# First-layer attention with keys on partitions: scores in column tiles, row sums by a matmul, reciprocals through DRAM

## Chip, cores and metric

One core of a Trainium2 chip runs the whole program. The metric is the device time of one execution in microseconds (us).

## The reference

Two transformer layers over x (16 batches x 64 tokens x 512). Only the first layer's cross-attention is touched:

```
q = rope(layernorm(x) @ Wq)          32 heads x 128
k = rope(ctx @ Wk), v = ctx @ Wv      8 key heads x 128, four query heads share one
logits = 30 * tanh((q . k) * 0.0884 / 30)          per batch 64 x 64
weights = softmax(where(mask, logits, -1e30))       the mask is the same for all rows and batches
x = x + (weights @ v) @ Wo
x = x + lora_experts(layernorm(x))                  first layer's FFN
x = x + attention2(layernorm(x), ctx)               16 heads x 96
x = x + dense(layernorm(x))
```

The given mask is true where a key is padding, and the reference keeps the logits where it is true. A row with no true entry gets equal weights.

## The kernel before

`plan()` writes one list of steps; each engine's program (`sync_program`, `gpsimd_program`, `scalar_program`, `vector_program`, `tensor_program`) walks the list in that order and does its own part of every step, so a wait on an engine holds everything that stands behind it in the list. A semaphore per PSUM bank says full and another free. Banks 0, 1, 6, 7 are a ring in the loop; bank 2 (PS) holds scores, bank 3 (PT) transposes, banks 4 and 5 (PA) the product with V.

Projections are done to nearly fp32 accuracy with three fp32r matmuls per product (`thrice`, lines 976 to 978): weights and activations are split in a high and a low part. A `split` step loads 256 KB of weights through one of four stage buffers (SP, line 519), writes the high part on ScalarE (line 603) and the low part on GpSimd (line 569). fp32 matmuls (scores, P·V) leave two records each in the trace.

The first layer's attention loop has NS = 32 steps s, each for two query heads (unit u = s // 2) and one half of the batch (s % 2, 8 batches). Per step:

- q0, 2 tiles of 12 matmuls with 512 columns (line 976 ff.); rope in three VectorE multiplications (lines 827, 828, 830) and a GpSimd addition (578) into `qb`;
- b0, scores: per batch a matmul of 64 columns, queries of two heads on the partitions (line 1031); tanh on ScalarE (645), mask on VectorE (847), exp on ScalarE (647), row sum, reciprocal and normalization on VectorE (852, 854, 856), all in `Eb`;
- c0: four 128x128 transposes (983) to PT and a ScalarE copy to `pTb`;
- d0, P·V: 8 matmuls with 64 rows in two row tiles (1050), 128 columns each, into the two PA banks; high part on ScalarE (603), low part on VectorE (865);
- e0: 4 tiles of 6 matmuls with Wo (976 ff.), each added to `xs` on VectorE (760).

The loop runs them in a software pipeline: iteration it issues b0(it-1), q0(it), d0(it-2), e0(it-3), c0(it-1), with splits, keys k0 and values v0 strewn in. Before the loop the first half of x and ctx (LO) is normalized, transposed and projected, then the second (HI). There the list reads: stats and rstd of HI (VectorE lines 778 to 800), q0(0), mask_bias (834 to 840), k0(0,1), transposes and values of HI.

```
for it in range(NS + 2):
    if 0 <= it - 1 < NS: stage("b0", it - 1, bank=2)
...
    if 0 < it < NS: q0(it)
...
    if 0 <= it - 2 < NS: d0(it - 2)
...
    if 0 <= it - 3 < NS: e0(it - 3)
...
    if 0 <= it - 1 < NS: stage("c0", it - 1, bank=3)
```

Of the kernel before, what the change touches and what calls it, by code (L numbers as in the profile page):

```python
# [7 lines left out]
NS = 32  # L8
# [54 lines left out]
def plan():  # L63
# [3 lines left out]
    def split(*name):  # L67
        step("split", *name)
# [28 lines left out]
    def q0(s):  # L97
        for n in range(2):
            stage("q0", s, n)

    def d0(s):
        for w in range(2):
            tile("d0", s, w, bank=4 + w)
        step("d0", s)

    def e0(s):
        for c in range(4):
            stage("e0", s, c)
# [12 lines left out]
    split("wq0", 0)  # L121
    split("wq0", 1)
# [18 lines left out]
    for it in range(NS + 2):  # L141
        if 0 <= it - 1 < NS:
            stage("b0", it - 1, bank=2)
        if it % 4 == 0 and it // 4 + 1 < 8:
            split("wk0", it // 4 + 1)
        if it % 8 == 1 and it // 8 + 1 < 4:
            for c in range(2):
                split("wv0", it // 8 + 1, c)
        if it % 2 == 0 and it // 2 + 1 < 16:
            split("wq0", it + 2)  # L150
        if it % 2 == 1 and it < NS:
            split("wo0", it - 1)
        if 0 < it < NS:
            q0(it)
        if it == NS + 1:
            k1(0, 0, 0)
        if 0 <= it - 2 < NS:
            d0(it - 2)
        if it % 2 == 1 and it + 2 < 32:
            split("wq0", it + 2)  # L160
        if 0 <= it - 3 < NS:
            e0(it - 3)
        if it % 2 == 0 and 2 <= it <= NS:
            split("wo0", it - 1)
        if it % 4 in (1, 2) and it // 4 + 1 < 8:
            stage("k0", it // 4 + 1, it % 4 - 1)
        if 3 <= it % 8 <= 6 and it // 8 + 1 < 4:
            for i in range(2):
                v0(it // 8 + 1, 2 * (it % 8 - 3) + i)
        if 0 <= it - 1 < NS:  # L170
            stage("c0", it - 1, bank=3)
        if it == NS - 2:
            split("wk1", 0, 0)
        if it == NS - 1:
            split("wv1", 0)
            split("wv1", 1)
        if it == NS:
            split("wq1", 0, 0)
            split("wq1", 0, 1)
        if it == NS + 1:  # L180
            split("wv1", 2)
            split("wq1", 0, 2)
            step("ffn_load")
# [33 lines left out]
    e0(NS - 1)  # L217
# [100 lines left out]
def program(nc, a, out):  # L318
# [18 lines left out]
    with ExitStack() as ctx:  # L337
# [9 lines left out]
        arena = sb("arena", [128, 10240])  # L347
# [3 lines left out]
        rtmp = [arena[:, 6144 + s * 512:6144 + (s + 1) * 512] for s in range(2)]  # L351
        K1 = [arena[0:96, j * 2048:(j + 1) * 2048] for j in range(4)]
        w1T = arena[:, 8192:10240].rearrange("p (k n) -> p k n", k=4)
# [7 lines left out]
        Ol = sb("Ol", [128, 2, 2, 512], f32r)  # L361
        Ohp, Olp = (O[:, :, :, :].rearrange("p s n t -> p s (n t)") for O in (Oh, Ol))
# [13 lines left out]
        mbias = sb("mbias", [128, 64])  # L376
        many = sb("many", [128, 1])
# [14 lines left out]
        with nc.sbuf_tensor("cTh", [128, 4, 1024], f32r) as cTh, nc.sbuf_tensor("cTl", [128, 4, 1024], f32r) as cTl:  # L392
# [5 lines left out]
        mids = [bank[:, 0:272].rearrange("p (i n) -> p i n", i=4) for bank in (PS, PT)]  # L398
        wk_home = [(WKh[:, :], WKl[:, :]), (WOh[:, 1, :], WOl[:, 1, :])]
        wk1_at = {(0, 0): 0, (1, 0): 1, (2, 0): 0, (0, 1): 0, (1, 1): 0, (2, 1): 0}  # L400
        wv1_home = [(WVh[:, 0:384], WVl[:, 0:384]), (WVh[:, 512:896], WVl[:, 512:896]),
                    (WOh[:, 2, 0:384], WOl[:, 2, 0:384]), (WOh[:, 0, 0:384], WOl[:, 0, 0:384])]
# [19 lines left out]
        s_msk, s_exp, s_sum, s_rec, s_nrm = (sem(n) for n in ("masked", "exp", "rowsum", "rowrec", "probs"))  # L422
        s_ohi, s_ohi1 = sem("o_hi"), sem("o_hi1")
        s_mb = sem("mask_bias")
# [836 lines left out]
```

## Time and profile before

| | |
|---|---|
| median of 3 runs | 926.53 us (925.81 to 926.71) |
| profiled execution | 922.79 us, span 921.0 us, granted TensorE clock 0.994 |
| TensorE matmul busy | 890.2 us, 97% |
| TensorE weight load busy | 757.1 us, 82% |
| VectorE, ScalarE, GpSimd busy | 583.4, 375.2, 270.5 us |
| HBM | 38.7 MB by SP's DMA queue |

Matmul records are pipelined: one of 512 columns lasts 0.39 us and the next starts 0.23 after it. The first layer's attention loop runs from about 43 to 579 us, its FFN to about 620, the second layer to the end. A granted clock of 1.00 is 2.4 GHz on TensorE.

### The profile page before, as it was taken

What the parts mean: (1) busy time and instruction counts of PE and PEld (TensorE: products, weight loads), DVE (VectorE), ACT (ScalarE), POOL (GpSimd) and SP (SyncE); (2) the same over time, 40 slices, a digit from 0 to 9 for tenths busy, and PEclk for the clock granted to TensorE, in tenths of its full rate; (3) what the DMA queues carried; (4) which work ended last, traced back from release to release, by engine and by line L of the source; (5) the groups of instructions that cost most, each with busy time, mean ns of one, the idle gap of its engine ahead of it and who ended that gap; (6) DMA issues with size and microseconds to landing.
All of it is one profiled execution on the core that took longest, in us unless ns stands there. A gap on an engine that the chain in (4) does not pass through costs nothing.

```text
span 921.0 us, 13308 instructions
## 1 busy us (share of the span) xinstructions
PE 890.2 (97%) x5144; PEld 757.1 (82%) x5144; DVE 583.4 (63%) x1035; ACT 375.2 (41%) x875; POOL 270.5 (29%) x212
## 2 busy tenths in 40 slices
PE   5889999999999999999999999799999999999998
PEld 5778888888888888888888888669987888888776
DVE  6886765876765876765877776753134454555684
ACT  4533222313222323222322223446576767766642
POOL 3263323533323533323433333100021211102132
PEclk9999999999999999999999999899999999999999
DMA  8021101211101211101111112100010110210002
GB/s 291 1 81 36 46 24 35 69 29 29 46 23 35 69 27 32 47 23 35 46 28 43 32 32 87 35 3 10 12 46 24 35 47 24 94 45 1 1 1 92
DMA packets 21888, 39.56 MB, mean 43 GB/s; under 512 B 2944, under 2 KB 3840, under 8 KB 21696
## 3 DMA queue, kind: packets, MB, share of 16 engines
q1 hardware_dynamic: 21824, 38.70, 13.9%
q8 instruction: 41, 0.67, 0.3%
q14 instruction: 23, 0.19, 0.1%
HBM read 36.60 MB, written 2.10 MB: 42 GB/s over the span
## 4 chain that ended last, share of the span: by engine, by line
PE 81%; DVE 7%; ACT 7%; issue 2%; POOL 1%; DMA 1%; SPq 0%; DVEq 0%; POOLq 0%
PE PB L976 20%; PE PB L978 19%; PE PB L977 19%; PE PB L1031 6%; PE PB L1122 5%; PE PB L1050 4%; PE PB L983 3%; ACT Eb L728 2%; PE PB L1137 2%; PE PB L1154 2%; DVE Ol L947 1%; ACT Oh L603 1%; DVE st L778 1%; DVE sm L929 1%; ACT qb L718 1%
## 5 line engine op out<-in xcount | busy, mean ns | idle before, releaser
L760 DVE TENSOR_TENSOR xs<-xs,PB 128x512 f32<-128x512 f32 x176 | 114.8, 682 | 35.6 <-PE PB L978 32.0
L976 PE MATMUL PB<-WOh,Oh 128*128 128x512 f32 x320 | 128.0, 400 | 0.0
L978 PE MATMUL PB<-WOh,Ol 128*128 128x512 f32 x320 | 125.0, 391 | 0.0
L977 PE MATMUL PB<-WOl,Oh 128*128 128x512 f32 x320 | 124.8, 390 | 0.0
L603 ACT ACTIVATE Oh<-PB 128x512 fp32r<-128x512 f32 (+2 forms) x160 | 71.0, 465 | 131.3 <-PE PB L1050 113.2
L578 POOL TENSOR_TENSOR qb<-qb,arena 128x512 f32<-128x512 f32 x64 | 82.9, 1295 | 108.2 <-DVE arena L830 108.2
L976 PE MATMUL PB<-xTh,WQh 128*128 128x512 f32 x256 | 102.8, 402 | 2.0 <-DVE xTl L807 2.0
L978 PE MATMUL PB<-xTh,WQl 128*128 128x512 f32 x256 | 100.0, 391 | 0.0
L977 PE MATMUL PB<-xTl,WQh 128*128 128x512 f32 x256 | 99.8, 390 | 0.0
L569 POOL TENSOR_TENSOR WOl<-stage,WOh 128x512 fp32r<-128x512 f32 (+1 forms) x43 | 54.8, 1276 | 144.4 <-ACT WOh L603 140.5
L569 POOL TENSOR_TENSOR WQl<-stage,WQh 128x512 fp32r<-128x512 f32 x44 | 59.9, 1364 | 98.6 <-ACT WQh L603 72.0
L847 DVE SCALAR_TENSOR_TENSOR Eb<-Eb,many,mbias 128x512 f32<-128x512 f32 x32 | 29.2, 913 | 81.2 <-ACT Eb L645 81.2
L976 PEld LDWEIGHTS PB<-WOh,Oh 128*128 128x128 f32 x320 | 60.0, 188 | 15.4
L603 ACT ACTIVATE pTb<-PB 128x512 f32<-128x512 f32 (+1 forms) x74 | 43.8, 592 | 65.7 <-PE PB L983 64.7
L978 PEld LDWEIGHTS PB<-WOh,Ol 128*128 128x128 f32 x320 | 60.1, 188 | 12.7
L977 PEld LDWEIGHTS PB<-WOl,Oh 128*128 128x128 f32 x320 | 60.1, 188 | 11.7
L983 PE MATMUL PB<-ident_sb,Eb 128*128 128x128 f32 x384 | 57.8, 275 | 11.1 <-DVE Eb L934 5.6
L947 DVE TENSOR_TENSOR Ol<-PB,Oh 96x256 fp32r<-96x256 f32 (+1 forms) x96 | 40.4, 421 | 41.8 <-ACT Oh L603 40.7
L1031 PE MATMUL PB<-arena,qb 128*128 128x64 f32 x512 | 60.8, 272 | 2.5 <-POOL qb L578 2.5
L728 ACT ACTIVATE Eb<-PB,sm 128x128 f32<-128x128 f32 x128 | 45.3, 366 | 43.5 <-DVE sm L929 43.5
L1031 PEld LDWEIGHTS PB<-arena,qb 128*128 128x128 f32 x512 | 59.7, 192 | 2.9 <-issue 2.9
L983 PEld LDWEIGHTS PB<-ident_sb,Eb 128*128 128x128 f32 x384 | 45.5, 141 | 19.0 <-DVE Eb L934 6.9
(152 smaller groups left out, 1892.0 us busy)
## 6 DMA issues: line engine op xcount, KB each, us to landing
stage<-in_wq SPq DMA_DIRECT2D x44, 256.0 KB, 2.6
stage<-in_wo SPq DMA_DIRECT2D x44, 256.0 KB, 2.6
stage<-in_wk SPq DMA_DIRECT2D x14, 256.0 KB, 2.6
arena<-in_ctxT SPq DMA_DIRECT2D x8, 256.0 KB, 5.7
xs<-in_x SPq DMA_DIRECT2D x8, 256.0 KB, 6.5
stage<-in_wv SPq DMA_DIRECT2D x8, 256.0 KB, 3.7
out<-xs SPq DMA_DIRECT2D x8, 256.0 KB, 2.0
arena<-in_w SPq DMA_DIRECT2D x1, 1024.0 KB, 5.2
```

The source lines that it names most:

```text
L569: e.tensor_tensor(lo, staged[:, n % 4, 0:cols], hi.bitcast(f32), ALU.subtract).then_inc(s_wlo)
L578: e.tensor_tensor(dst, dst, tmp, ALU.add).then_inc(s_radd)
L603: return e.activation(dst, src, ACT.Copy)
L728: last = e.activation(Eb[:, e2, cols], PS[:, cols], ACT.Exp, bias=mx[:, bb:bb + 1], accum_out=rs[:, bb:bb + 1])
L760: e.tensor_tensor(xs[:, i, :], xs[:, i, :], PB[b][:, :], ALU.add).then_inc(free[b])
L947: last = e.tensor_tensor(dl, src, dh.bitcast(f32), ALU.subtract)
L976: e.matmul(dst, Ah, Bh, start=(k == 0), stop=False)
L977: e.matmul(dst, Ah, Bl, start=False, stop=False)
L978: return e.matmul(dst, Al, Bh, start=False, stop=(k == n - 1))
L983: last = e.transpose(dst[:, c * 128:(c + 1) * 128], src[:, c * 128:(c + 1) * 128], ident[:, :])
L1031: last = e.matmul(PS[:, c * 64:(c + 1) * 64], qb[:, s % 2, c * 128:(c + 1) * 128], kT[j % 2][:, 512 * hf + 64 * c:512 * hf + 64 * c + 64], ...
L1122: last = e.matmul(PB[b][:, :], W[:, m, r], H[:, c, cols], start=(n % 12 == 0), stop=(n % 12 == 11))
```

## The change

A step is now a unit of four query heads, all that share one key head, and one half of the batch: NU = 16. Each unit has two halves h of four batches.

- b0: the key block is the stationary operand, the queries of four heads (256 columns) move. The result has 64 key rows; two batches fill the two column tiles of 64, four matmuls a half. Softmax's numerator then lies with keys on partitions, as P·V wants it, so c0 is gone.
- The mask is folded in two tables on the host-transposed mask: `ropeq` (rope times 1 or 0, so that logits become 0 if no key is kept) and `keep` (1 or 0 per key and query), which GpSimd multiplies after exp. Their making (`mask_tables`) uses a matmul with ones into bank 3, ahead of q0(0).
- sum0: four matmuls a half with a stationary `ones` of 32 columns and 128 moving columns, each in its own column tile of 32, into PT; VectorE takes the reciprocal of 128 x 128; SP writes the four useful rows for each of two batch parities to DRAM (`recs`), waits, and reads them back spread over 64 partitions (`rsum`); VectorE multiplies (norm0).
- d0: per half 4 matmuls of 256 columns. e0: one tile per 128 tokens sums four heads: 48 matmuls a unit as before in two steps, with 4 additions to xs instead of 8.
- Four weight slots instead of three for Wq and Wo; `w1T` gets room of its own. Four wq0 splits stand ahead of the first k0 (before two), and wk0(1), wv0(1), wo0(0..3) ahead of the loop.

```diff
@@ plan()
-    split("wq0", 0)
-    split("wq0", 1)
+    for n in range(4):
+        split("wq0", n)
     stage("k0", 0, 0)
...
     step("rstd", 0, 4)
-    q0(0)
-    step("mask_bias")
+    tile("many", bank=3)
+    step("mask_tables")
+    for n in range(4):
+        q0(0, n)
     stage("k0", 0, 1)
+    split("wk0", 1)
     normed(0, HI, [lambda i=i: v0(0, i) for i in range(5, 8)], [lambda: v0(0, 4)])
...
+    for c in range(2):
+        split("wv0", 1, c)
+    for n in range(4):
+        split("wo0", n)
+    for u in range(NU):
+        def queries(n):
+            if u + 1 < NU:
+                q0(u + 1, n)
+                if u % 2 == 0 and u + 2 < NU:
+                    split("wq0", 2 * u + 4 + n)
+        def outputs(c):
+            if u:
+                e0(u - 1, c)
+        b0(u, 0)
+        queries(0)
+        if u == NU - 1:
+            k1(0, 0, 0)
+        b0(u, 1)
+        queries(1)
+        sum0(u, 0)
+        outputs(0)
+        sum0(u, 1)
+        outputs(1)
+        norm0(u, 0)
+        queries(2)
+        norm0(u, 1)
+        queries(3)
+        d0(u, 0)
+        outputs(2)
+        outputs(3)
+        if u and u % 2 == 0:
+            for n in range(4):
+                split("wo0", 2 * u + n)
+        d0(u, 1)
+        j, hf = u // 2 + 1, u % 2
+        if j < 8:
+            stage("k0", j, hf)
...
     ring[0:0] = [4, 5]
-    e0(NS - 1)
+    for c in range(4):
+        e0(NU - 1, c)
@@ sync_program
+                elif kind == "sum0":
+                    u, h = k
+                    n, s = 2 * u + h, h
+                    sp.wait_ge(*read("sum0", u, h))
+                    if u:
+                        sp.wait_ge(s_in_rec[s], 32 * u)
+                    for bb in range(2):
+                        e.dma_start(recs[s, bb], rec[16 * bb:128:32, s, :]).then_inc(s_out_rec[s], 16)
+                    sp.wait_ge(s_out_rec[s], 32 * (u + 1))
+                    if u:
+                        sp.wait_ge(s_nrm, n - 1)
+                    for bb in range(2):
+                        e.dma_start(rsum[s][64 * bb:64 * bb + 64, :].rearrange("p (g x) -> p g x", g=4),
+                                    recs[s, bb].unsqueeze(0).broadcast_to([64, 4, 128])).then_inc(s_in_rec[s], 16)
@@ gpsimd_program
+                elif kind == "b0":
+                    u, h = k
+                    n = 2 * u + h
+                    E3 = E0[n % 4].rearrange("p (c t) -> p c t", c=8)
+                    pool.wait_ge(s_mb, 4)
+                    pool.wait_ge(s_exp, n + 1)
+                    e.tensor_tensor(E3, E3, keep[:, :].unsqueeze(1).broadcast_to([128, 8, 64]), ALU.mult).then_inc(s_msk)
@@ vector_program
+                elif kind == "mask_tables":
+                    dve.wait_ge(s_mask, 16)
+                    dve.wait_ge(s_rope, 16)
+                    e.tensor_copy(keep[:, :], mask8).then_inc(s_mb)
+                    dve.wait_ge(*done("many"))
+                    e.tensor_scalar(many[:, :], PT[:, 0:64], 1.0, None, ALU.min).then_inc(free[3])
...
+                elif kind == "sum0":
+                    u, h = k
+                    dve.wait_ge(*done("sum0", u, h))
+                    if u:
+                        dve.wait_ge(s_out_rec[h], 32 * u)
+                    e.reciprocal(rec[:, h, :], PT[:, 0:128]).then_inc(free[3])
+                elif kind == "norm0":
+                    u, h = k
+                    E = E0[(2 * u + h) % 4]
+                    dve.wait_ge(s_in_rec[h], 32 * (u + 1))
+                    e.tensor_tensor(E, E, rsum[h], ALU.mult).then_inc(s_nrm)
@@ tensor_program
+                elif kind == "mask_tables":
+                    pe.wait_ge(s_one, 1)
+                    pe.wait_ge(s_mb, 1)
+                    e.matmul(PT[:, 0:64], pTb[:, 0, 0:128], keep[:, :], start=True, stop=True).then_inc(full[3])
                 elif kind == "b0":
-                    for c in range(8):
-                        last = e.matmul(PS[:, c * 64:(c + 1) * 64], qb[:, s % 2, c * 128:(c + 1) * 128],
-                                        kT[j % 2][:, 512 * hf + 64 * c:512 * hf + 64 * c + 64], start=True, stop=True)
+                    for c in range(2):
+                        for r in range(2):
+                            b8 = 4 * h + 2 * c + r
+                            last = e.matmul(PS[64 * r:64 * r + 64, 256 * c:256 * c + 256],
+                                            kT[j % 2][:, 512 * hf + 64 * b8:512 * hf + 64 * b8 + 64],
+                                            qb[:, u % 2, 256 * b8:256 * b8 + 256], start=True, stop=True)
-                elif kind == "c0":
-                    s, = k
-                    pe.wait_ge(s_nrm, s + 1)
-                    turn(PT, Eb[:, s % 2, :], 4).then_inc(full[b])
+                elif kind == "sum0":
+                    for c in range(4):
+                        last = e.matmul(PT[32 * c:32 * c + 32, 0:128], ones[:, :],
+                                        E0[n % 4][:, 128 * c:128 * c + 128], start=True, stop=True)
                 elif kind == "d0":
+                    for c in range(2):
...
+                        for r in range(2):
...
+                            last = e.matmul(PA[r][:, 256 * c:256 * c + 256], V[rows, i, c0:c0 + 128],
+                                            E0[n % 4][rows, 256 * c:256 * c + 256], start=True, stop=True)
                 elif kind == "e0":
+                    for n in range(4):
+                        last = thrice(PB[b][:, :], n, 4, O4h[:, n, rows], O4l[:, n, rows], *wo_home[n])
```

## Rows read from the trace of the kernel before

**Rows 1.** The windows of the trace: stretch, its us, busy us of each engine (instructions), granted clock, DMA
```profile
160.00:240.00 80.00, 80.00 (x465) 67.32 (x464) 59.84 (x86) 22.23 (x41) 34.48 (x26) 1.00 0.15 43
...
580.00:600.00 20.00, 14.54 (x86) 12.50 (x85) 12.51 (x42) 11.79 (x20) 3.48 (x3) 0.83 0.14 40
```

**Rows 2.** Timeline of one step of the loop, TensorE: start us, us, instruction
```profile
302.79 0.39 PE L978 MATMUL PB<-xTh,WQl 128*128 128x512 f32 x1
...
303.11 1.16 PE L1050 MATMUL PB<-pTb,arena 64*128 64x128 f32 x16
...
304.20 0.50 PE L976 MATMUL PB<-WOh,Oh 128*128 128x512 f32 x1
...
304.54 0.39 PE L977 MATMUL PB<-WOl,Oh 128*128 128x512 f32 x1
...
309.55 0.39 PE L978 MATMUL PB<-WOh,Ol 128*128 128x512 f32 x1
...
309.78 0.60 PE L983 MATMUL PB<-ident_sb,Eb 128*128 128x128 f32 x4
...
310.22 1.90 PE L1031 MATMUL PB<-arena,qb 128*128 128x64 f32 x16
...
311.92 0.48 PE L976 MATMUL PB<-xTh,WQh 128*128 128x512 f32 x1
```

**Rows 3.** Timeline, second layer's scores, 96 rows, 128 columns
```profile
701.07 1.06 PE L1137 MATMUL PB<-arena,qb 96*128 96x128 f32 x8
701.88 0.48 PE L1122 MATMUL PB<-xTh,WQh 128*128 128x512 f32 x1
```

**Rows 4.** Chain that ended last, eight records of 512 columns
```profile
607.27 3.63 PE PB L1087 x8
```

**Rows 5.** Groups by line, busy us, mean ns: softmax instructions
```profile
L856 DVE TENSOR_TENSOR Eb<-Eb,sm 128x512 f32<-128x512 f32 x32 | 45.6, 1426 | 1.1
...
L854 DVE RECIPROCAL sm<-sm 128x8 f32<-128x8 f32 x32 | 6.5, 203 | 1.1
...
L932 DVE RECIPROCAL sm<-sm 128x4 f32<-128x4 f32 x32 | 5.7, 178 | 50.8 <-ACT Eb L728 50.8
```

**Rows 6.** The page's part 6, DMA issues: KB each, us to landing
```profile
stage<-in_wq SPq DMA_DIRECT2D x44, 256.0 KB, 2.6
...
arena<-in_ctxT SPq DMA_DIRECT2D x8, 256.0 KB, 5.7
...
out<-xs SPq DMA_DIRECT2D x8, 256.0 KB, 2.0
```

**Rows 7.** Timeline, TensorE's waits at the start
```profile
25.74 0.47 PE L976 MATMUL PB<-xTh,WQh 128*128 128x512 f32 x1 [1.78 <-DVE xTl L807]
...
42.34 0.66 PE L983 MATMUL PB<-ident_sb,Eb 128*128 128x128 f32 x4 [1.11 <-DVE arena L830]
...
56.15 1.97 PE L1031 MATMUL PB<-arena,qb 128*128 128x64 f32 x16 [2.31 <-POOL qb L578]
```

**Rows 8.** Timeline, VectorE at the start
```profile
15.98 1.20 DVE L796 TENSOR_TENSOR lnb<-lnb 128x4 f32<-128x4 f32 x1
...
34.28 0.16 DVE L800 SCALAR_TENSOR_TENSOR lnb<-mv,lnb 128x4 f32<-128x4 f32 x1
...
38.60 0.20 DVE L834 CAST mbias<-mask 128x64 f32<-128x64 uint8 x1
```

**Rows 9.** Timeline, GpSimd at the start
```profile
14.64 2.52 POOL L569 TENSOR_TENSOR WQl<-stage,WQh 128x512 fp32r<-128x512 f32 x2
```

**Rows 10.** Timeline, TensorE: first matmul after the last e0, and the FFN's wait
```profile
578.94 0.39 PE L976 MATMUL PB<-cTh,WKh 128*128 128x512 f32 x1
...
593.05 1.09 PE L983 MATMUL PB<-ident_sb,Eb 128*128 128x128 f32 x4 [4.27 <-ACT Eb L624]
```

**Rows 11.** Timeline, VectorE, additions after the last e0
```profile
579.95 2.47 DVE L760 TENSOR_TENSOR xs<-xs,PB 128x512 f32<-128x512 f32 x4
```

More of the change, by code:

```diff
@@ L95, in v1, with q0, b0, sum0 @@
         stage("v1", w, i)
[L97 to L101, printed above, removed]
-        for w in range(2):
[L103 to L108, printed above, removed]
+    def q0(u, n):
+        stage("q0", u, n)
+    def b0(u, h):
+        stage("b0", u, h, bank=2)
+    def sum0(u, h):
+        stage("sum0", u, h, bank=3)
+    def norm0(u, h):
+        step("norm0", u, h)
+    def d0(u, h):
+        for w in range(2):
+            tile("d0", u, h, w, bank=4 + w)
+        step("d0", u, h)
+    def e0(u, c):
+        stage("e0", u, c)
     split("wk0", 0)
@@ L346, in program @@
         xTl = sb("xTl", [128, 4, 1024], f32r)
-        arena = sb("arena", [128, 10240])
+        arena = sb("arena", [128, 8192])
+        with nc.sbuf_tensor("W3", [128, 4, 512], f32r) as W3:
+            more = [W3[:, n, :] for n in range(4)]
+        w1T = sb("w1T", [128, 4, 512])
         kT = [arena[:, s * 1024:(s + 1) * 1024] for s in range(2)]
@@ L636, in scalar_program @@
                     else:
[L637 removed]
+                        act.wait_ge(*done("d0", 4 * (pr - 2) + 3, 1, 1))
                     b = bank_of("v0", pr, i)
@@ L1047, in tensor_program @@
+                    for c in range(2):
+                        i = 4 * hf + 2 * h + c
+                        pe.wait_ge(*read("v0", j // 2, i))
                         for r in range(2):
-                            pe.wait_ge(*opened("d0", s, r))
+                            pe.wait_ge(*opened("d0", u, h, r))
                             rows = slice(64 * r, 64 * r + 64)
-                            last = e.matmul(PA[r][:, c * 128:c * 128 + 128], V[rows, 4 * hf + c, c0:c0 + 128],
-                                            pTb[rows, e2, c * 128:(c + 1) * 128], start=True, stop=True)
@@ L1059, in tensor_program @@
-                    pe.wait_ge(*read("d0", s, 1))
-                    pe.wait_ge(*lo_ready("wo0", 2 * u + 1))
-                    for n in range(2):
-                        slot = (2 * u + n) % 3
-                        last = thrice(PB[b][:, :], n, 2, Oh[:, e2, n, rows], Ol[:, e2, n, rows], WOh[:, slot, :], WOl[:, slot, :])
+                    pe.wait_ge(*read("d0", u, c // 2, 0))
+                    pe.wait_ge(*read("d0", u, c // 2, 1))
+                    pe.wait_ge(*lo_ready("wo0", 4 * (u // 2) + 3))
```

241 lines of the change are left out of this document (109 added, 132 removed).

## The prediction, made before the result was known

> **What bounds the kernel.** I read the windows first. In the first layer's attention loop TensorE is busy 80.00 of 80.00 us at granted clock 1.00, VectorE 59.84, GpSimd 34.48, ScalarE 22.23 [rows 1]. Matmuls are pipelined, so a busy row proves no peak, but there is no gap: every start follows the one before. The loop is priced by start-to-start times on TensorE, and time taken from another engine brings nothing there. So I read one step of the timeline [rows 2]. From 304.54 to 309.55 lie 22 starts of 512-column fp32r matmuls, 0.228 each. The step's fp32 stages are: P·V (L1050) 303.11 to 304.20, 1.09 us for 16 records; four transposes (L983) 309.78 to 310.22, 0.44; scores (L1031) 310.22 to 311.92, 1.70 for 16 records. Each fp32 matmul leaves two records, so half a matmul is a record below. Entering P·V costs 0.32 - 0.23 = 0.09 (302.79 to 303.11), leaving it 0.34 - 0.23 = 0.11 (304.20 to 304.54).
>
> **The loop, part by part.** A unit (4 heads, one half of the batch) replaces two steps; there are 16. The projections, 48 q0 and 48 e0 matmuls a unit, stay, and so do keys and values. Removed from TensorE per unit: scores 3.40, transposes 0.88, P·V 2.18, entries and exits 2 x (0.09 + 0.11) = 0.40, and leaving the scores about 0.09 each, which I take as 0.18 like the entry: together 7.04 us.
>
> Added: scores are 8 matmuls, 16 records, of 256 columns and 64 outputs, pairs of which sit in different column halves of the array. No row of before shows a column tile. Prices of 256 full-array columns: 128 columns took (701.88 - 701.07)/8 = 0.101 a record [rows 3], 512 took 3.63/8 = 0.454 [rows 4], so 256 stand near 0.227, or 0.213 counted from two passes at 2.4 GHz. If the two tiles of a pair run one after another, 16 records are 3.63. If they run together as the row tiles of P·V do: those are 0.068 a record, 0.136 a pair for 128 columns, where one takes 0.101 to 0.107, so a pair costs its stream plus 0.03. A 256-column pair is then 0.243 and the unit's scores 1.95. I take that; the lower end is one stream with nothing added, 1.7. The row sums are 16 records of 128 columns in four column tiles of 32: four at a time 0.107 + 3 x 0.03 = 0.2, so 0.8 a unit; ends 0.45 and 1.7 (serial, 16 x 0.107). P·V becomes 16 records of 256 columns in row tiles, 0.243 a pair, 1.95; ends 1.75 and 2.18. Six small stages stand alone between projections instead of four: 6 x (0.09 + 0.11) = 1.2; ends 0.6 and 2. The sum is 5.9 against 7.04: 1.14 us less a unit, **18 us less** over 16 units.
>
> The Trainium skill ("TensorEngine Tiling (Array Packing)", Key Properties) says that changing the tiling mode drains TensorE. The 0.20 for P·V's way in and out agrees with a short drain. The skill's "TensorE: Matmul & The Clock Gate", Part 3, gives for three column tiles 2.38 times the speed, which speaks for the pairs, but also says that a weight load overlaps a running matmul only when their row groups differ. The column tiles share all rows. By that rule the pairs would not run together; the untiled fp32r loads here do overlap matmuls on the same rows, as loads busy 67.32 beside matmuls busy 80.00 of 80 us show [rows 1].
>
> **VectorE, ScalarE and GpSimd in the loop.** VectorE loses the mask, the sums and half the additions into xs, and gets much lighter; ScalarE loses the copies of the transposes; GpSimd gets two more multiplications of about 1.3 to 1.5 us a unit. All cost nothing while TensorE covers them. New is the chain that each half unit must run before its P·V. The reciprocal now has 128 columns: from 4 to 8 columns it grew 25 ns [rows 5], 6.25 a column, so about 0.95 us. Then two DMAs out, a wait on SP, two DMAs in, each way one issue of 0.4 behind the other and 2.0 or 2.6 to land [rows 6]: 2.4 + 3.0, then a multiplication of up to 1.43 [rows 5]. With some 0.1 per hand-over the chain is near 8 us from the start of the reciprocal. The timetable of a unit, with 12 x 0.228 = 2.73 for a tile of q0 or e0, 1.2 for a score stage with its ways in and out and 0.6 for a row sum: scores to 1.2, q0 to 3.9, scores to 5.1, q0 to 7.8, row sum to 8.4, e0 to 11.1, second row sum to 11.7, then e0, q0, q0 to 19.9, where TensorE wants the first probabilities. VectorE has the rope of the second q0 to do (3 instructions, 2.1 us, to 10.0), so the reciprocal ends at 11.0 and the probabilities are ready at about 18.0: 1.9 us of slack. The second half has 5 us of slack, its DMAs queued on SP behind the first's. The tight place is the bank PT: the first reciprocal frees it at 11.0 and TensorE wants it at 11.1. I add 0.15 us a unit for the times that it is late, **2.5 us**. SP's weight loads stand behind the DMAs in its order; they are issued about half a unit before their split and stay hidden.
>
> **The start.** This speaks against the change. Before, TensorE begins the first queries at 25.74 [rows 7] while VectorE still computes the statistics of the second half. Now a small matmul for the mask stands ahead of q0 in TensorE's order and waits for VectorE's cast of the mask, which stands behind those statistics. They end at 34.44 (before, the cast ran at 38.60, behind two ropes) [rows 8]. They also slip: small VectorE instructions took 1.20 instead of 0.16 while GpSimd split weights [rows 8, 9], and two more query weights are split there; two instructions held for 1.2 us each give about 2.1. So q0 starts near 37.1, 11.4 later. TensorE has then stood for over 10 us. After a wait of 4.27 us in the FFN four transposes took 1.09 where the loop has 0.60 [rows 2, 10], and 580 to 600 shows clock 0.83 in the mean: part of it at 1.2 instead of 2.4 GHz, 20 x 0.17 = 3.4 us lost if nothing of it were idle [rows 1]; I add 2. The 1.11 us wait at 42.34 [rows 7] goes. That makes 12.5.
>
> In the first unit no e0 stands between the small stages, only q0, and six weight splits (wv0 twice, wo0 four times) stand ahead of its softmax on ScalarE and GpSimd. The first two can begin only when the last v0 is done, just before the first scores. GpSimd takes 1.3 to 1.5 each; the third and fourth wo0 need the stage buffers that these two free, and then a DMA of 2.6 [rows 6]. So ScalarE reads the first scores only at about 8.3 us after they start, where TensorE wants their bank at 4.4 (4.0 lost). The second row sums wait for GpSimd (2.3), P·V for the DMAs (0.6 and 2.1), q0 for the split of x (0.6): 9.6, and 2 for the clock again. Before loses 2.31 and 0.2 here [rows 7]: net 9. **The start costs 21.5 us.**
>
> **The end of the loop.** The last unit has no queries to cover the chain: P·V waits 1.8, and the first e0 waits 1.8 for bank 4, which VectorE reads just then. Against that e0(15) is one block of 10.9 us, so LayerNorm's statistics run beside it, and the additions end 0.8 us after TensorE's last e0 matmul, not 3.5 after (582.42 against 578.94) [rows 10, 11]; of the 4.27 wait [rows 10] 2.7 go, and of the slow clock around it, at most 3.4, I take 2.4. Net **-1.5**. The second layer is not touched.
>
> **Sum:** -18 + 2.5 + 21.5 - 1.5 = +4.5 us. The profiled execution took 922.79 (span 921.0), 3.7 under the median of 926.53; I carry the difference over to the median: **931.0**.
>
> **Rivals.** (a) The pack is perfect and the drains are small: scores 1.7, sums 0.45, P·V 1.75, ways in and out 1.2 give 5.1 a unit, 31 us less, and the kernel is faster: -31 + 2.5 + 21.5 - 1.5 = -8.5, 918.0. Faster begins where a unit's small stages cost below 7.04 - 22.5/16 = 5.6. For it: the loads of 64 and 32 columns may be shorter. Against: P·V's pairs fell short of it in before. (b) The column tiles run one after another: 3.63 + 1.7 + 1.95 + 1.2 = 8.5, 1.44 more a unit, +23 over the loop, and the longer unit frees PT in time: 23 + 21.5 - 1.5 = +43, 969.5. It is also the case of a change that does not do what it says. (c) The DMA chain is longer than its cover. The ctxT loads, queued several deep, took 5.7 [rows 6]; were each way 2 us longer, 4 against 1.9 us of slack, the first P·V of a unit would wait 2 us, 32 over the loop: 963.0. Against: these are small transfers on a queue that is mostly empty.
>
> **Numbers.** Forecast 0.40 (some 925 to 940), (a) 0.27, (b) 0.20, (c) 0.13. Below 0.2%, some 1.9 us, no difference can be told. Faster: (a) and a little of the forecast, 0.31; within 0.2%: 0.10; slower 0.59. The range takes (a) to its lower part and (b) and (c) to near their middle: 914 to 967.
>
> **What would show it.** Two score matmuls of one pair starting within 0.05 us, and the stage of 8 records ending in about 1.0 us: right; in 1.8: (b). TensorE idle from 26 to about 37 on the cast of the mask, with a lower clock behind it. P·V without a wait on the probabilities in the middle units; 2 us there is (c). The unit should take TensorE about 1.1 us less than two steps did. If the q0 matmuls start before the cast, the start is wrong, and the time falls by ten.

## The result, and the profile after

The changed kernel takes 945.29 us (median of 4 runs, 944.26 to 945.57), against 926.62 for the kernel before beside it: ratio 1.0201, 95% interval 1.0183 to 1.0219. It is slower by 18.7 us. Its profiled execution took 945.55 us, span 943.7, granted clock 0.975. The forecast was made against the profiled execution of before, which at granted clock 0.994 was 3.7 us under its median (span 921.0), and there the difference is 22.7 us; the rest of this document accounts for those 22.7, of which the forecast had 4.5.

The windows of the kernel after answer to [rows 1] (stretch, its us, busy us of TensorE, weight loads, VectorE, ScalarE, GpSimd, then granted clock, DMA share, GB/s):

```profile
20.00:40.00 20.00, 7.91 (x40) 6.62 (x40) 13.55 (x39) 8.26 (x16) 1.73 (x5) 0.69 0.28 105
80.00:100.00 20.00, 14.03 (x67) 10.93 (x67) 10.26 (x15) 3.86 (x8) 5.84 (x5) 0.83 0.16 54
240.00:320.00 80.00, 80.00 (x429) 60.57 (x428) 44.75 (x65) 16.72 (x31) 33.13 (x26) 1.00 0.14 47
560.00:580.00 20.00, 13.59 (x68) 8.69 (x64) 5.09 (x7) 7.55 (x14) 11.51 (x10) 0.83 0.21 63
600.00:620.00 20.00, 15.84 (x76) 13.69 (x75) 9.66 (x38) 9.13 (x16) 3.49 (x3) 0.69 0.14 40
```

The middle of the loop is as tight as before: TensorE 80.00 of 80.00 us at clock 1.00. The loss lies in the three places where TensorE is not busy: the start, the first unit, and the end of the loop with the FFN behind it. In all of these the granted clock is low as well.

**The loop.** The timeline of one unit, TensorE (start us, us, instruction), answers to [rows 2]:

```profile
301.63 1.08 PE L1107 MATMUL PB<-qb,arena 128*64 128x256 f32 x8
302.65 0.50 PE L1046 MATMUL PB<-xTh,WQh 128*128 128x512 f32 x1
...
309.27 0.39 PE L1048 MATMUL PB<-xTh,WQl 128*128 128x512 f32 x1
309.59 0.43 PE L1117 MATMUL PB<-pTb,ones 128*32 128x128 f32 x8
309.95 0.50 PE L1046 MATMUL PB<-WOh,Oh 128*128 128x512 f32 x1
310.28 0.39 PE L1047 MATMUL PB<-WOl,Oh 128*128 128x512 f32 x1
...
321.64 1.13 PE L1132 MATMUL PB<-pTb,arena 64*128 64x256 f32 x8
322.71 0.50 PE L1046 MATMUL PB<-WOh,Oh 128*128 128x512 f32 x1
...
335.28 1.08 PE L1107 MATMUL PB<-qb,arena 128*64 128x256 f32 x8
```

A score stage of 8 records takes 302.65 - 301.63 = 1.02 us, a row sum 309.95 - 309.59 = 0.36, a P·V half 322.71 - 321.64 = 1.07. Each stage has the same way in (309.27 to 309.59 is 0.32 where a projection takes 0.23) and out (309.95 to 310.28 is 0.33), 0.2 in all, six times a unit. Asked for in windows of 0.05 us, the eight score records start two at a time, at 301.63, 301.90, 302.12 and 302.33: this is the sign that the forecast asked for. That makes 2 x (1.02 + 0.36 + 1.07) + 1.2 = 6.10 us, against 7.04 removed. The whole unit takes 335.28 - 301.63 = 33.65 us. In before four units (eight steps) took 138.10 us by the same timeline, 34.53 each. So the loop gained 0.88 us a unit, 14 over 16 units. It was forecast at 18, less 2.5 for a bank that would come late; that bank never came late in units 1 to 14, where TensorE has no wait at all.

**The waits of TensorE** in the kernel after answer to [rows 7] and [rows 10] (in brackets the idle time before the instruction, and what ended it):

```profile
21.48 1.27 PE L1053 MATMUL PB<-ident_sb,Eb 128*128 128x128 f32 x8 [1.37 <-ACT Eb L694]
...
35.76 0.66 PE L1098 MATMUL PB<-keep,pTb 128*128 128x64 f32 x2 [10.73 <-DVE keep L907]
...
67.91 1.50 PE L1107 MATMUL PB<-qb,arena 128*64 128x256 f32 x8 [3.13 <-ACT Eb L721]
76.69 0.43 PE L1117 MATMUL PB<-Eb,ones 128*32 128x128 f32 x8 [2.82 <-DVE rec L922]
83.20 1.13 PE L1132 MATMUL PB<-Eb,arena 64*128 64x256 f32 x8 [0.39 <-DVE Eb L927]
89.91 2.57 PE L1132 MATMUL PB<-Eb,arena 64*128 64x256 f32 x8 [5.58 <-DVE Ol L935]
...
568.00 1.98 PE L1107 MATMUL PB<-qb,arena 128*64 128x256 f32 x8 [4.46 <-ACT pTb L721]
570.47 0.66 PE L1117 MATMUL PB<-pTb,ones 128*32 128x128 f32 x8 [0.50 <-POOL pTb L648]
579.99 0.49 PE L1132 MATMUL PB<-pTb,arena 64*128 64x256 f32 x2 [1.45 <-DVE pTb L927]
589.28 0.50 PE L1046 MATMUL PB<-WOh,Oh 128*128 128x512 f32 x1 [1.41 <-DVE Ol L935]
600.33 0.40 PE L1046 MATMUL PB<-cTh,WKh 128*128 128x512 f32 x1
...
608.82 3.52 PE L1153 MATMUL PB<-qb,pTb 128*128 128x68 f32 x16
615.31 1.09 PE L1053 MATMUL PB<-ident_sb,Eb 128*128 128x128 f32 x4 [2.97 <-ACT Eb L694]
```

The start: 1.37 us at 21.48, 10.73 for the mask, and the 12 projection matmuls behind it start 0.43 apart instead of 0.23 (2.4 us). The first unit: 3.13 + 2.82 + 0.39 + 5.58, and 0.39 at 61.77, make 12.3 us of waits. The windows give the clock at most 20 x 0.09 = 1.8 us in 60 to 80 (granted 0.91) and 20 x 0.17 = 3.4 in 80 to 100; by the records that ran slowly it is 1.6 (the scores at 67.91 took 1.50 instead of 1.08, and projections behind them 0.43 apart) and 3.0 (P·V 2.57 instead of 1.13, and projections again). Less the waits that before has there (1.78, 1.11, 2.31 [rows 7], 0.22 and 0.19) these are 25.8. The end of the loop: 4.46 + 0.50 + 1.45 + 1.41 = 7.8 us of waits, and 2.4 for the clock, as experiment 3 will show. The first matmul behind the last e0 starts at 600.33, where before it did at 578.94 [rows 10], 21.4 later. The parts, 25.8 - 14.1 + 10.2, make 21.9, so they are known to about 0.5. From there to the FFN's transposes it takes 14.98 us (615.31) where before took 14.11 (593.05 [rows 10]), and by the first projection of the second layer the distance has grown from 21.4 to 22.8; at the end it is 22.7.

### The profile page after: what moved, and what is told of

Same layout as the page of the kernel before. It is cut to its first block, busy times and chain, and to the rows that moved or that the text cites. A ratio compares the mean times of both kernels' runs of the same rounds, so it can differ in the third digit from the quotient of the medians.

```text
span 943.7 us, 12573 instructions
## 1 busy us (share of the span) xinstructions
PE 887.4 (94%) x4762; PEld 703.6 (75%) x4762; DVE 498.1 (53%) x908; ACT 359.1 (38%) x843; POOL 305.1 (32%) x248
## 4 chain that ended last, share of the span: by engine, by line
PE 78%; ACT 8%; DVE 7%; issue 3%; DMA 3%; POOL 1%; SPq 1%; POOLq 0%; DVEq 0%; ACTq 0%
PE PB L1046 21%; PE PB L1047 19%; PE PB L1048 19%; PE PB L1202 5%; PE PB L1132 3%; PE PB L1107 3%; PE PB L1053 2%; ACT Eb L797 2%; PE PB L1217 2%; PE PB L1234 2%; ACT Oh L673 1%; DVE Ol L1017 1%; PE PB L1117 1%; ACT qb L787 1%; DVE sm L999 1%
## 5 line engine op out<-in xcount | busy, mean ns | idle before, releaser
L829 DVE TENSOR_TENSOR xs<-xs,PB 128x512 f32<-128x512 f32 x112 | 76.6, 685 | 77.1 <-PE PB L1048 74.2
L1048 PE MATMUL PB<-WOh,Ol 128*128 128x512 f32 x256 | 100.4, 392 | 0.0
L1047 PE MATMUL PB<-WOl,Oh 128*128 128x512 f32 x256 | 100.4, 392 | 0.0
L899 DVE TENSOR_TENSOR qb<-PB,ropeq 128x512 f32<-128x512 f32 x64 | 44.0, 688 | 100.8 <-PE PB L1048 100.8
L1047 PE MATMUL PB<-xTl,WQh 128*128 128x512 f32 x192 | 76.8, 400 | 0.0
L1048 PE MATMUL PB<-xTh,WQl 128*128 128x512 f32 x192 | 75.9, 395 | 0.0
L673 ACT ACTIVATE WQh<-stage 128x512 fp32r<-128x512 f32 x36 | 22.7, 629 | 117.3 <-DMA stage<-in_wq 93.8
L935 DVE TENSOR_TENSOR Ol<-PB,Oh 128x512 fp32r<-128x512 f32 x64 | 41.2, 686 | 26.8 <-ACT Oh L673 26.3
L1046 PEld LDWEIGHTS PB<-xTh,WQh 128*128 128x128 f32 x192 | 36.9, 192 | 19.8 <-issue 12.5
L1053 PE MATMUL PB<-ident_sb,Eb 128*128 128x128 f32 x256 | 39.3, 279 | 10.1 <-DVE Eb L1004 5.5
L673 ACT ACTIVATE arena<-PB 128x256 f32<-128x256 f32 (+3 forms) x56 | 26.2, 475 | 53.6 <-PE PB L1048 53.1
```

The source lines that it names most:

```text
L673: return e.activation(dst, src, ACT.Copy)
L829: e.tensor_tensor(xs[:, i, :], xs[:, i, :], PB[b][:, :], ALU.add).then_inc(free[b])
L899: e.tensor_tensor(dst, src, table[:, 0:1, :].broadcast_to([128, 8, 64]), ALU.mult)
L1046: e.matmul(dst, Ah, Bh, start=(k == 0), stop=False)
L1047: e.matmul(dst, Ah, Bl, start=False, stop=False)
L1048: return e.matmul(dst, Al, Bh, start=False, stop=(k == n - 1))
```

## The experiments

The kernel before runs beside each one (926.4 to 926.8 us, but 923.5 in experiment 8). The times are medians of four runs, of two in experiments 7 and 8; the rows are of one execution each. Unless said otherwise an experiment is the changed kernel with one edit.

**1. The mask ahead of the second half's statistics.**

```diff
@@ plan()
     step("rope_table")
+    step("mask")
...
         step("v0_move", 0, i)
+    tile("many", bank=3)
+    step("mask_tables")
     step("ctx", 1)
...
-    step("mask")
...
-    tile("many", bank=3)
-    step("mask_tables")
     for n in range(4):
         q0(0, n)
```

> The changed kernel (945.3 us) with the mask's load and tables moved ahead of the second half's statistics, so that TensorE need not wait for the cast. Theory of the start: TensorE stood 10.7 us on the cast and then ran 12 matmuls 0.43 instead of 0.23 apart, 2.4 us; both go, 12 to 13 us less, about 933, and the granted clock of 20 to 40 us rises from 0.69 to 1.00. Rival: the wait only moves on to the second half's transposes or the rope, less than 4 us are gained.

It took 935.24 us, ratio 1.0102 [1.0072, 1.0133]: 10.1 us less than the change, where 12 to 13 were expected. The timeline of TensorE at the start:

```profile
26.53 0.41 PE L1098 MATMUL PB<-keep,pTb 128*128 128x64 f32 x2 [1.77 <-DVE keep L907]
```

The wait falls from 10.73 to 1.77. So it was the place of the cast in VectorE's order, not its own length, that held TensorE. The granted clock of 20 to 40 rose from 0.69 to 1.00, but in 60 to 80 it is 0.76 here and 0.91 in the change. The profiled execution, 932.02, was the fastest of the four and 13.5 us under the change's; why the other three gained less is not seen.

**2. The six splits of the first unit.** Two `wv0` and four `wo0` splits move from ahead of the loop into the first unit, behind its scores and to its end.

```diff
@@ plan()
-    for c in range(2):
-        split("wv0", 1, c)
-    for n in range(4):
-        split("wo0", n)
     for u in range(NU):
...
         b0(u, 1)
+        if u == 0:
+            for c in range(2):
+                split("wv0", 1, c)
         queries(1)
...
-        if u and u % 2 == 0:
+        if u % 2 == 0:
             for n in range(4):
```

> The changed kernel with the six weight splits (wv0(1) twice, wo0 four times) moved from ahead of the loop into the first unit, behind its scores. Theory: they stood before the first tanh on ScalarE; the 3.13 us wait of the second scores goes, with some 2.5 us of slow clock, and part of the 2.8 us wait of the second row sums: 5 to 8 us less, 937 to 940. Rival: the first unit is bound by its DMA chain, and what is gained at the scores is waited for at P.V: under 2 us.

939.57 us, ratio 1.0144 [1.0118, 1.0170], 5.7 less. The 3.13 us wait of the second scores is gone. The row sums still wait 2.82, so that wait is no matter of the splits, and the P·V wait is 5.17. In the kernel after they come from VectorE's order:

```profile
75.68 0.96 DVE L922 RECIPROCAL rec<-PB 128x128 f32<-128x128 f32 x1
```

The second row sum needs the bank PT, the reciprocal that frees it ends at 76.64, and it stands behind the rope of the second q0. GpSimd had done its part of the second half at 73.97 already. No run moved this reciprocal.

**3. The splits at the end of the loop.** The splits of `wq1` (three) and `wv1` (one) are written in unit 14, before the softmax of unit 15. The experiment moves them to unit 15.

```diff
@@ plan()
-        if u == NU - 2:
+        if u == NU - 1:
             split("wq1", 0, 0)
```

> The changed kernel with the four splits for the second layer (wq1 three times, wv1(2)) moved from the end of unit 14 to the end of unit 15. Theory: the 4.46 us wait of the last unit's second scores came from ScalarE standing on their loads ahead of the tanh; it goes with about 2.5 us of slow clock: 5 to 7 us less, 938 to 940. Rival: the wait comes back at the row sums or P.V of the last unit, or the second layer waits for its weights: under 2 us.

940.87 us, ratio 1.0157 [1.0132, 1.0182], 4.4 less, where 5 to 7 were expected. The wait of 4.46 us is gone; in its place the row sums wait 1.16 us for GpSimd. From unit 14's scores to the first matmul behind the last e0 it takes 62.68 us (533.21 to 595.89) instead of 68.88 (531.45 to 600.33): 6.2 less, of which 4.46 + 0.50 - 1.16 = 3.8 are waits and 2.4 the clock (1.00 in 560 to 580, where the change has 0.83). That the profiled execution gains less in all (4.6 in spans) is due to the first unit, whose steps are the same but which ended 1.75 us later here (unit 1's scores at 101.50 instead of 99.75). ScalarE in the kernel after shows what stood ahead of the last tanh:

```profile
563.23 0.63 ACT L673 ACTIVATE WQh<-stage 128x512 fp32r<-128x512 f32 x1 [1.50 <-DMA stage<-in_wq]
...
566.94 0.52 ACT L673 ACTIVATE W<-stage 128x384 fp32r<-128x384 f32 x1 [0.18 <-DMA stage<-in_wv]
567.37 0.58 ACT L721 ACTIVATE pTb<-PB 128x512 f32<-128x512 f32 x1
```

Each split takes ScalarE 0.6 us, but it waits for its load, and the tanh, whose scores have long been ready, waits behind all four: it ends 0.05 us before TensorE goes on at 568.00.

**4. SP's order.** My first theory for the 5.58 us at the second P·V: two weight loads stand behind the reciprocals' DMAs on SP, ScalarE's splits wait for them, and the high part of O stands behind the splits. SP alone is given another order here:

```diff
@@ sync_program
-            for kind, *k in steps:
+            order = list(steps)
+            for u in range(0, NU - 2, 2):
+                for n in (2, 3):
+                    st = ("split", "wq0", 2 * u + 4 + n)
+                    order.remove(st)
+                    order.insert(order.index(("sum0", u, 0)), st)
+            for kind, *k in order:
```

> The changed kernel with SP alone reordered: in every even unit the loads of the third and fourth query weights are issued ahead of the reciprocals' DMAs instead of behind them. Theory: in the first unit ScalarE stood on these loads ahead of P.V's copy, and P.V's second half waited 5.58 us for its bank; most of it and 3 to 4 us of slow clock go: 5 to 9 us less, 936 to 940. Rival: P.V's second half then waits for its own probabilities at nearly the same time: 2 to 3 us less. Middle units: no change, since TensorE waits for nothing there.

945.41 us, ratio 1.0208 [1.0182, 1.0233]: nothing gained of the 5 to 9 expected. ScalarE and VectorE in this experiment, and the second P·V:

```profile
86.62 1.09 ACT L679 ACTIVATE Oh<-PB 128x512 fp32r<-128x512 f32 x2 [0.37 <-PE PB L1138]
...
90.13 1.29 DVE L941 TENSOR_TENSOR Ol<-PB,Oh 128x512 fp32r<-128x512 f32 x2
...
90.97 2.58 PE L1138 MATMUL PB<-Eb,arena 64*128 64x256 f32 x8 [4.38 <-DVE Ol L941]
```

The high part is done at 87.71, but VectorE begins the low part only at 90.13, so here VectorE alone makes the wait of 4.38 us. (That it was 5.58 in the change is not SP's doing either: experiment 7, with SP's order unchanged, has 4.27.) The theory falls as the main cause. What VectorE does there in the kernel after:

```profile
86.06 0.97 DVE L927 TENSOR_TENSOR Eb<-Eb,arena 128x512 f32<-128x512 f32 x1 [0.92 <-DMA arena<-recs]
...
88.36 0.68 DVE L902 TENSOR_TENSOR arena<-PB,ropeq 64x512 f32<-64x512 f32 x1
89.07 1.29 DVE L935 TENSOR_TENSOR Ol<-PB,Oh 128x512 fp32r<-128x512 f32 x2
```

The subtraction that frees the two banks of P·V (L935) stands behind the second normalization, which waits for its DMA until 86.06, and behind a rope. (In the kernel after ScalarE's high part ends as late, at 89.10; the two ended together there.) In the later units e0 of the unit before lies between the two P·V halves and covers this; unit 0 has no e0.

**5. The second P·V half later.** This tests that reading: the half moves behind k0 and v0, and VectorE's order stays as it is up to there.

```diff
@@ plan()
-        d0(u, 1)
         j, hf = u // 2 + 1, u % 2
...
                 v0(pr, 2 * m + i)
+        d0(u, 1)
+        if pr < 4:
             if m == 3 and pr + 1 < 4:
```

> The changed kernel with P.V's second half moved behind the keys and values of its unit. The order of SP was not the cause of the first unit's 5.6 us wait. Theory now: VectorE frees P.V's banks only after the second normalization, which waits for its DMA, and a rope; with 5.6 us of keys and values between the two P.V stages the wait is covered, and with it 3 to 4 us of slow clock go: 7 to 10 us less, 935 to 938. Rival: the next unit's scores or the e0 tiles then wait for P.V's results: under 3 us.

934.55 us, ratio 1.0103 [1.0079, 1.0126], 10.7 less. The wait is gone: unit 1's scores start at 94.18 instead of 99.75, 5.6 us earlier. A slow stretch stays in the first unit, now from 78 to 83 us. The rest is in the loop: the half now lies against the next scores, and two small stages side by side share a way in and out. Scores to scores:

```profile
94.18 1.08 PE L1108 MATMUL PB<-qb,arena 128*64 128x256 f32 x8
...
127.68 1.08 PE L1108 MATMUL PB<-qb,arena 128*64 128x256 f32 x8
```

This is 33.50 us a unit instead of 33.65, 2.2 from unit 1 to unit 14. 5.6 + 2.2 = 7.8, of the 8.4 by which the span is shorter (935.3 against 943.7). The profiled execution was the slowest of the four (937.04); what the others gained beyond it is not seen.

**6. No round trip through DRAM.** SP's four reciprocal DMAs and VectorE's wait for them are left out, and the probabilities are multiplied by `keep` again in place of the reciprocals: this kernel leaves out the division by the row sums.

```diff
@@ sync_program, sum0
-                    sp.wait_ge(*read("sum0", u, h))
...
+                    pass
@@ vector_program, norm0
-                    dve.wait_ge(s_in_rec[h], 32 * (u + 1))
-                    e.tensor_tensor(E, E, rsum[h], ALU.mult).then_inc(s_nrm)
+                    dve.wait_ge(s_msk, 2 * u + h + 1)
+                    e.tensor_tensor(E.rearrange("p (c t) -> p c t", c=8), E.rearrange("p (c t) -> p c t", c=8),
+                                    keep[:, :].unsqueeze(1).broadcast_to([128, 8, 64]), ALU.mult).then_inc(s_nrm)
```

> The changed kernel without the reciprocals' four DMAs per half and without the waits on them; the probabilities are multiplied by the 0/1 table once more instead of by the reciprocals (the division by the row sums is left out). Theory: in units 1 to 14 the round trip costs TensorE nothing, their length stays 33.6 us; in the first unit most of the 5.6 us wait of P.V and in the last the 1.45 us go, with 4 us of slow clock: 933 to 938. Rival: contention of the small DMAs with weights or VectorE's waits cost in every unit: more than 12 us less, and shorter units.

940.23 us, ratio 1.0168 [1.0134, 1.0201], 5.1 less, where 7 to 12 were expected. TensorE from scores to scores, its first P·V of the last unit, and VectorE's multiplication for it:

```profile
128.64 1.08 PE L1096 MATMUL PB<-qb,arena 128*64 128x256 f32 x8
...
162.28 1.08 PE L1096 MATMUL PB<-qb,arena 128*64 128x256 f32 x8
...
575.06 1.13 PE L1121 MATMUL PB<-pTb,arena 64*128 64x256 f32 x8 [1.45 <-DVE pTb L915]
...
574.32 1.29 DVE L915 TENSOR_TENSOR pTb<-pTb,keep 128x512 f32<-128x512 f32 x2
```

The unit takes 33.64 us, as in the change: in the middle of the loop the chain through DRAM costs nothing. The gain is all in the first unit, whose second P·V waits 1.95 us instead of 5.58: unit 1's scores start 4.8 us earlier (94.99), and unit 14's also 4.8 (526.69). At the end nothing is gained. The last unit's P·V waits 1.45 us as in the change, though there are no DMAs: the multiplication (L915 here, L927 in the kernel after) stands on VectorE right behind an addition to xs, which waits for its e0 tile. So this wait is VectorE's order and not the chain. No run moved the addition.

**7. Another order of the tiles.** The score products go A, A, B, B (A and B the two column tiles) instead of A, B, A, B.

```diff
@@ tensor_program, b0
-                    for c in range(2):
-                        for r in range(2):
+                    for r in range(2):
+                        for c in range(2):
```

> The changed kernel with the order of the four score matmuls of a half turned: the two of one column tile back to back, then the two of the other. Theory of the pairs: neighbours in different column tiles stream together (8 records in 1.02 us); turned, at best one neighbouring pair in three does, and 8 records take 1.5 to 1.7 us: 32 halves give 15 to 22 us more, 960 to 967. Rival: a 256-column record costs 0.13 us in any order, since 64 outputs load fast: no change.

945.91 us, ratio 1.0220 [1.0188, 1.0252]: no change, and the stage still takes 302.38 - 301.36 = 1.02 us. Its records also start two at a time (301.36, 301.63, 301.85, 302.06):

```profile
301.36 1.09 PE L1107 MATMUL PB<-qb,arena 128*64 128x256 f32 x8
302.38 0.50 PE L1046 MATMUL PB<-xTh,WQh 128*128 128x512 f32 x1
```

Either the tiles work side by side in any order, or they don't work side by side at all and a small product is cheap. The next run tells the two apart.

**8. One tile alone.** From unit 1 on every score product writes rows 0 to 63, every row sum rows 0 to 31, and every P·V product reads rows 0 to 63.

```diff
@@ tensor_program
-                            last = e.matmul(PS[64 * r:64 * r + 64, 256 * c:256 * c + 256],
+                            q = 64 * r if u == 0 else 0
+                            last = e.matmul(PS[q:q + 64, 256 * c:256 * c + 256],
...
-                        last = e.matmul(PT[32 * c:32 * c + 32, 0:128], ones[:, :],
+                        q = 32 * c if u == 0 else 0
+                        last = e.matmul(PT[q:q + 32, 0:128], ones[:, :],
...
-                            rows = slice(64 * r, 64 * r + 64)
+                            rows = slice(64 * r, 64 * r + 64) if u == 0 else slice(0, 64)
```

> The price of the new products by itself, from unit 1 on: all four score products of a half write rows 0 to 63 of the score bank (one column tile instead of two), all four row sums of a half write rows 0 to 31 of their bank (one tile instead of four), and all four P.V products of a half read rows 0 to 63 of the probabilities and of V (one row tile instead of two). The same number of instructions of the same sizes. It leaves out the scores of half of the keys, the sums of three heads in four and the P.V of half of the rows (unit 0 alone is whole). Theory tiles (different tiles run beside each other, and that is why 8 score records take 1.02 us, 0.128 a record of 256 columns, and 4 sums 0.36): with one tile the eight score records take 1.7 to 2.0 us, the sums 0.4 to 0.5, P.V 1.7 to 2.0, so +1.5 to 2 us a unit, 24 to 32 us over 15 units: 969 to 977 us. Rival small (an fp32 record with 64 rows of output and 256 columns costs this by itself, wherever it is put, as the turned order that changed nothing suggests): 1.02, 0.36 and 1.07 as before, unit 33.65, 943 to 948 us.

1013.62 us, ratio 1.0965 [1.0877, 1.1052], 68 us more than the change. One unit:

```profile
292.35 1.94 PE L1108 MATMUL PB<-qb,arena 128*64 128x256 f32 x8
294.23 0.50 PE L1046 MATMUL PB<-xTh,WQh 128*128 128x512 f32 x1
...
301.99 1.06 PE L1119 MATMUL PB<-Eb,ones 128*32 128x128 f32 x8
302.98 0.50 PE L1046 MATMUL PB<-WOh,Oh 128*128 128x512 f32 x1
...
315.29 1.99 PE L1134 MATMUL PB<-Eb,arena 64*128 64x256 f32 x8
317.21 0.50 PE L1046 MATMUL PB<-WOh,Oh 128*128 128x512 f32 x1
...
330.68 1.94 PE L1108 MATMUL PB<-qb,arena 128*64 128x256 f32 x8
```

Scores 1.88 instead of 1.02, row sums 0.99 instead of 0.36, P·V 1.92 instead of 1.07; with two of each a unit that is 4.7 us, and the unit grew from 33.65 to 38.33. (The range that I wrote down, 969 to 977, was too low: I had counted one half a unit, and 0.4 to 0.5 for the row sums.) The score records now start one by one, at 292.35, 292.62, 292.84 and so on, 0.22 apart, where in the change two start together. So tiles do work side by side, and they are what makes the new stages cheap. In this kernel score products and row sums of one tile also write the same place of their bank again, which could be thought to hold them up; P·V's products write two different banks as before and slow down at the same price. The price per record follows from the differences: (1.88 - 1.02)/4 = 0.215 us for 256 columns, (0.99 - 0.36)/6 = 0.105 for 128, (1.92 - 1.07)/4 = 0.213 for P·V's 256. In these three stages the cost is that of the fullest tile's records at that price, and 0.15 to 0.2 on top.

**9. The four moves together**: experiments 1, 2, 3 and 5 in one kernel.

> The changed kernel with four moves at once: mask tables early, first unit's splits later, the last unit's four splits later, P.V's second half behind keys and values. Theory: the losses stand in different places and add: 945.3 - 10 - 6 - 4.5 - 8 = 917, faster than the kernel before (926.8) by 1%, since the loop itself is 14 us shorter. Rival: they share slow clock and cover, and the sum stays above 926.

It took 913.93 us (911.95 to 916.51), ratio 0.9876 [0.9846, 0.9906]. It is faster than both kernels, by 12 us than before and by 31.4 than the change (917 was expected); the four gains alone add up to 10.1 + 5.7 + 4.4 + 10.7 = 30.9. What is left of TensorE's waits between 20 us and the end of the FFN, of those over 1.5 us, is 1.77 for the mask, 2.82 for the first unit's row sums and 2.97 in the FFN. A unit takes 33.47 us by the starts of its scores (111.88 and 145.35).

## Why the prediction was wrong in size

It said slower by 4.5 us; it was 22.7 in spans and 18.7 in medians. The measured time lies in the range, and slower was the likelier side, but most of the loss was not in the sum. The steps that failed are two waits that it did not have, the tanh's at the end of the loop and the bank's at the first unit's second P·V, and a gain of 5.1 us in the FFN that did not come.

- **The loop: right, slightly too good.** The prices of the stages were taken from P·V's row tiles and held within a tenth: 1.95 a unit for scores (measured 2.04), 0.8 for row sums (0.72), 1.95 for P·V (2.14), 1.2 for ways in and out (1.2). Together 6.10 instead of 5.9, and 14 us gained instead of 15.5 net. The term that was off is P·V and scores: I had priced a pair as its stream plus 0.03, where a tile streams at 0.213 a record and each stage pays some 0.2 once. (The price of 0.227 came from [rows 4], which I called full-array; the trace has those records as 64*128, a row tile. One tile alone gives 0.213 to 0.215 in experiment 8.) Rival (b), tiles one after another, is what experiment 8 makes, 68 us slower than the change; it is not this kernel. Rival (a)'s prices were not reached by a fifth (6.1 against 5.1).
- **The DMA chain: right.** The reciprocal took 0.95 us (forecast 0.95). The first reciprocal of a unit starts at 311.82 and the probabilities are ready at 319.09, 7.3 us later (forecast near 8), 2.5 before TensorE begins P·V at 321.64, and no P·V of units 1 to 14 waits. Rival (c) did not happen, and experiment 6 puts its price in the loop at nothing. The allowance of 2.5 us for the bank of the row sums was not needed in these units.
- **The mask at the start: right.** q0 was to start near 37.1, 11.4 later than before, and started at 36.17, 0.4 behind the mask's matmul and 10.4 later than before; the wait was over 10 us, and the clock behind it was low (2.4 us, forecast 2). The terms written down, 11.4 + 2 - 1.1, add up to 12.3 and not to the 12.5 that was carried on. Experiment 1 returns 10.1.
- **The first unit: a wait was missed.** The forecast had P·V wait for the DMAs only (0.6 and 2.1, measured 0.39 and hidden). It did not follow VectorE's order past the second normalization to the subtraction that frees P·V's banks: 5.58 us. Experiment 5 shows that the wait goes when the stage is covered, the rows of experiment 4 that VectorE's order holds it and not SP's; experiment 6 leaves 1.95 of it, so more than half of it hangs on the DMAs that the second normalization, ahead of the rope, waits for. Other waits of the unit were forecast at 4.0 and 2.3 and measured 3.13 and 2.82. The second is right by luck: it was to be for GpSimd and was for the bank PT, which the rope on VectorE kept. As the low clock took 4.6 instead of 2 and before's own waits come off, the whole start cost 25.8 instead of 21.5.
- **The end of the loop: a wait was missed, and it cost most.** The forecast looked only at what P·V and e0 wait for: 1.8 and 1.8, measured 1.45 and 1.41. The first is luck too: it was to be the bare chain through DRAM, and experiment 6 has the same 1.45 without the chain. The forecast did not look at what the splits for the second layer, moved ahead of the last unit's softmax in ScalarE's order, do to the tanh: 4.46 us, 0.50 behind it, and 2.4 by the clock. Experiment 3 shows all three. With that the end cost 10.2 instead of 3.6.
- **The FFN: 5.1 us were claimed that were not to be had.** The additions do end 0.8 us after TensorE's last e0, as I wrote, but that frees VectorE, and the gate's arithmetic on VectorE (L955 to L978) can begin only when TensorE has done its 16 records (L1153 now, L1073 before): in before they end at 586.82 + 1.96 = 588.78 and the gate's first copy starts at 589.47, so at most 0.7 us of VectorE's lead could count. Even of that little was left. Experiment 1 shows the place at full clock (TensorE, then VectorE, then GpSimd):

```profile
596.85 1.96 PE L1153 MATMUL PB<-qb,pTb 128*128 128x68 f32 x16
602.95 1.09 PE L1053 MATMUL PB<-ident_sb,Eb 128*128 128x128 f32 x4 [4.14 <-ACT Eb L694]
...
599.05 0.59 DVE L957 TENSOR_TENSOR qb<-qb 128x64 f32<-128x64 f32 x1
599.56 1.03 DVE L958 TENSOR_TENSOR qb<-qb 128x64 f32<-128x64 f32 x1
...
598.29 1.26 POOL L625 TENSOR_TENSOR WKl<-stage,WKh 128x512 fp32r<-128x512 f32 x1 [1.97 <-issue]
```

  The gate begins on VectorE as soon as TensorE is done, but beside GpSimd's two weight splits its small products take 0.59 and 1.03 us, where the change, whose gate starts as those splits end, has 0.22 for either. (That GpSimd is what slows them is read from their times alone; no run moved the splits.) TensorE's wait is 4.14 instead of 4.27. In the change the 16 records take 3.52 us instead of 1.96, at a granted clock of 0.69 in 600 to 620; the wait is shorter there, 2.97, because TensorE itself is late. Net this is +1.3 instead of -5.1.

**The ledger of the forecast against the spans:** loop +1.4, start +4.3, end of the loop +6.6 (10.2 instead of 3.6), FFN +6.4, 18.7 in all less the 0.5 by which the parts overshoot: the 18.2 between 4.5 and 22.7.

**The tiles and the drain.** The traces speak on the sentences of the Trainium skill that the forecast cites. Column tiles that share all their rows did run side by side: 1.02 instead of 1.88 us for two tiles, 0.36 instead of 0.99 for four. The rule of the Trainium skill ("TensorE: Matmul & The Clock Gate", Part 3), that a weight load overlaps a running matmul only on other row groups, would by itself have forbidden it; here the measurement decides against it. The same part's 2.38 for three tiles fits between the 1.84 for two and the 2.75 for four here, fixed part of the stage included. The Trainium skill ("TensorEngine Tiling (Array Packing)", Key Properties) says that a change of the tiling mode drains TensorE. On this the rows are divided, and the forecast's 0.20 was too much to say for it. For it: a small stage is entered 0.09 slower than a projection, and in before the full-array transposes are entered at a projection's pace, 0.23 from 309.55 to 309.78 [rows 2]. Against it: the way out costs 0.09 behind before's full-array scores too, where the tiling does not change,

```profile
312.24 0.39 PE L977 MATMUL PB<-xTl,WQh 128*128 128x512 f32 x1
```

0.32 from 311.92 [rows 2] instead of 0.23; and where in experiment 5 scores in column tiles follow P·V in row tiles directly, P·V takes 1.06 us (126.62 to 127.68), no more than the 1.07 of the change. So of the 0.2 only the 0.09 of the way in can be a drain, and no run separates it.

## What to carry to other kernels

When a change rearranges a pipeline, read its first and last round one engine at a time, in that engine's own order: a stage that the middle hides (a split that waits for its load, a subtraction behind a rope) is bare where the next stage's work doesn't exist yet or any more. Here the middle was forecast to 1.4 us and the ends lost more than twice what it gained; four moves in the order of steps turned +2.0% into -1.2%. And before the length of a wait is booked as a gain, look which of the engines that feed it would end last without it: here the lead of one was worth 0.13 us of 2.7.

## What the runs showed that I had not expected

- The order in which the score products of a half are issued made no difference: A, A, B, B took 1.02 us as A, B, A, B did, its records starting in pairs as well, where all on one tile took 1.88. How TensorE gets the second tile going while two products of the first are still ahead of it is left open; I made no run on it.
- The granted clock costs about as much as some of the waits. In the change it was low behind the waits of 10.73, 3.13, 5.58 and 4.46 us (0.69 in 20 to 40, 0.91 in 60 to 80, 0.83 in 80 to 100 and 560 to 580), but the low stretch in the FFN is not tied to one wait: of kernels with the same work there, the change and experiments 3, 4, 5, 6, 7 and 9 had the 16 gate records at 3.52 us, and experiments 1, 2 and 8 at 1.96, in the one profiled execution of each. What decides between them stays open.
